# Moving one block's shared chunks across a tile run, and its next routing behind them

## The chip, the cores and the metric

The kernel runs on one core of a Trainium2 chip. The metric is the device time of one execution in microseconds (us). Five engines take part: TensorE (PE, matrix products), VectorE (DVE), ScalarE (ACT), GpSimd (POOL; here it issues the indirect DMAs) and SyncE (SP; it issues the plain DMAs). Each runs its own program in order, and they meet only through semaphores.

## The reference

Input x has 2 x 1024 tokens of 256 features, all in float32. Six steps follow each other; LN is a layer norm without gain:

```
x = x + 0.5 * moe0(LN(x))      # feed-forward 0 (f = 0)
x = x + rwkv_block(LN(x))      # mixing
x = x + 0.5 * moe0(LN(x))      # f = 1, same weights as f = 0
x = x + 0.5 * moe1(LN(x))      # f = 2
x = x + linear_attention(LN(x))
x = x + 0.5 * moe1(LN(x))      # f = 3

def moe(x):                    # moe0: 8 experts, top 2, width 176, softmax scores
    scores = f(x @ gate_w)     # moe1: 32 experts, top 6, width 96, sigmoid scores
    routed = sum over the chosen experts e of w_e * ((silu(x @ wg[e]) * (x @ wu[e])) @ wd[e])
    shared = (silu(x @ sg) * (x @ su)) @ sd      # width 352 in moe0, 192 in moe1
    return routed + shared
```

So the routing of f = 2 for a token needs everything that f = 1 adds to that token: its shared part and both of its routed parts.

## The kernel before, in words

**Data.** The tokens are 16 tiles of 128, in 4 blocks of 512 (NB = 4, NT = 4). XT holds x in on-chip memory throughout. Each feed-forward has two parts:

- The *shared* part is computed in *chunks*: 3 per block for f = 0 and 1 (SH0), 2 per block for f = 2 and 3. For one chunk TensorE does `gate_up` (L794, 12 matmuls of 128x512, matmul at L817), ScalarE `silu` (L1375), VectorE `prod` (L2037), ScalarE `hidden` (L1381), VectorE `low_hidden` (L2044), and TensorE `down` (L820, 12 matmuls, L829). Each operand is split into a high and a low half, which is why there are so many steps. When a block's last `down` is done, VectorE adds it into XT (`finish`, L2049, instruction at L2061), which raises the semaphore CK.sum.
- The *routed* part works on *pages*. For each block the router makes statistics (`stats`), normalised rows (`rows`), a transposition (`turn`, L757), logits (L1026), scores (`score`, L1366), the chosen experts (`chosen`, L1891), ranks (L774) and slots (`slots`, L1932). POOL then scatters the rows into DRAM pages by slot (`scatter_tile`, L626; one indirect DMA per tile and choice, so 8 per block for f = 1 and 24 for f = 2). Pages are sorted by expert. The *tile run* (`tiles`, on TensorE L864) loads pairs of pages (20 pairs for f = 1), multiplies them with their expert's weights and writes them to DRAM. It can start only when every block is scattered. POOL gathers the results (`gather`, L645) and VectorE adds them into XT (`gathered`, L2072).

**The order around the change** is written out by hand, engine by engine.

1. *Mixing.* After its last step stands a drain, the list DRAIN (L125): the 9 shared chunks of f = 1 of blocks 0, 1 and 2 (`LATE = 3` blocks). Between chunks the routing of f = 1 for blocks 2 and 3 is done. Block 3's slots come after the sixth chunk.
2. *Tile run of f = 1.* TensorE waits for the sum of block 2 (L1338). Beside the pairs the engines route blocks 0 and 1 for f = 2 (`route_ahead`, `route_between`, `route_beside`) and VectorE gathers blocks 0, 1 and 2. At pair 19 VectorE makes the f = 2 statistics of block 2. SyncE loads five groups of the f = 2 expert weights at pairs 4 to 8 (`next_weights`, L567); these groups lie over memory that the mixing has finished with.
3. *`prepare2`.* The 3 held chunks of block 3 run between the steps of block 2's routing. VectorE then makes block 2's slots, adds block 3's sum, gathers block 3, makes block 3's statistics, and the 8 shared chunks of f = 2 run between the steps of block 3's routing.
4. *Tile run of f = 2.* SyncE waits for all scatters (L494) before the first page load.

POOL's own order (L721 to L744) is: gathers of f = 1 with the scatters of tiles 0 to 4 of f = 2 between them, then the scatters of tiles 5 to 15; the scatter of a block's first tile waits for the block's slots.

The chunks that run inside the mixing or its drain are of kind "s0" and those behind the tile run of kind "d0"; the kind chooses the buffers of S and HL only, which for "d0" lie over the expert weights of f = 0 and 1.

## Time and profile before

| | us |
|---|---|
| median of 3 runs | 1507.77 (1500.41, 1507.77, 1521.20) |
| the profiled execution | 1497.55 |
| its span in the profile | 1495.7 |
| TensorE busy in the span | 1178.6 (79%) |
| VectorE busy | 743.8 (50%) |
| POOL busy | 596.8 (40%) |
| ScalarE busy | 536.0 (36%) |

The span is what the profile shows of the profiled execution, and the other times are read inside it, in us from its start. A busy share is an average over all stages and says nothing of a single one. In a row of the timeline the bracket at the end is the time that the engine was idle before, and what released it; "remote" there is a release that the profile can't lay to a recorded instruction.

### The profile page before, as it was taken

Reading aid. Unit: us, or ns where it says so; the run is one execution under the profiler, and the core shown is the slowest. Engines: PE = TensorE matmul, PEld = TensorE weight load, DVE = VectorE, ACT = ScalarE, POOL = GpSimd, SP = SyncE. Lnnn points to the kernel's source line nnn. Section 1 sums busy time; section 2 is a strip of 40 time slices with the busy share of each in tenths; the row PEclk is TensorE's granted clock in tenths of the full one; section 3 lists DMA queues with packets and bytes.
Section 4 is the critical chain, followed back from the end, with each engine's and each line's share of the span. In section 5 each row is a group of like instructions: output and inputs, shape, how many; then the busy total and the mean of one; then the engine's idle time right before and its main releaser. Section 6 shows DMA issues by size and latency. Waiting matters only on the chain.

```text
span 1495.7 us, 20198 instructions
## 1 busy us (share of the span) xinstructions
PE 1178.6 (79%) x6031; PEld 960.0 (64%) x6031; DVE 743.8 (50%) x2333; ACT 536.0 (36%) x1012; POOL 596.8 (40%) x579
## 2 busy tenths in 40 slices
PE   4799988979989898854768998897755436988884
PEld 4677755666778676633557987875434225978784
DVE  5553465564546536413445555678644214633443
ACT  2323344554533234321413433442303115644442
POOL 3661352211124213674550155662453730045554
PEclk9789999998989999865868999898875667998897
DMA  9523439400002573331426687760121212676676
GB/s 331 211 72 107 143 96 308 141 1 0 1 29 107 206 260 119 117 114 64 173 76 216 195 241 237 219 191 4 60 79 41 105 53 63 198 208 205 204 223 191
DMA packets 125302, 209.81 MB, mean 140 GB/s; under 512 B 15296, under 2 KB 104768, under 8 KB 123328
## 3 DMA queue, kind: packets, MB, share of 16 engines
q1 hardware_dynamic: 100624, 141.38, 28.7%
q0 software_dynamic: 24576, 67.14, 14.4%
q8 instruction: 56, 0.92, 0.3%
q14 instruction: 46, 0.38, 0.1%
HBM read 129.29 MB, written 101.19 MB: 154 GB/s over the span
## 4 chain that ended last, share of the span: by engine, by line
PE 48%; DVE 18%; issue 13%; another core or an unknown queue 10%; ACT 6%; POOL 3%; DMA 1%; SPq 0%; DVEq 0%; POOLq 0%; ACTq 0%
PE ps L910 15%; PE ps L932 6%; PE ps L877 5%; PE ps L817 4%; PE ps L829 4%; PE ps L889 3%; PE ps L1093 2%; PE ps L1100 2%; ACT xnt L1360 1%; PE ps L927 1%; PE ps L1244 1%; DVE HL L2047 1%; POOL xd L638 1%; PE ps L925 1%
## 5 line engine op out<-in xcount | busy, mean ns | idle before, releaser
L653 POOL DMA_INDIRECT G<-yd,slot_of x256 | 253.1, 989 | 424.6 <-issue 189.3
L638 POOL DMA_INDIRECT xd<-xnt,slot_of x256 | 251.4, 982 | 224.4 <-DVE slot_of L1986 136.9
L910 PE MATMUL ps<-WE,xT 128*128 x1016 | 200.7, 343 | 5.6 <-issue 3.9
L2102 DVE TENSOR_TENSOR hid<-hid,ps 128x192 f32<-128x192 f32 (+2 forms) x168 | 65.4, 389 | 247.9 <-ACT hid L1551 198.1
L910 PEld LDWEIGHTS ps<-WE,xT 128*128 128x128 f32 x1016 | 174.0, 202 | 9.9 <-issue 9.7
L1522 ACT ACTIVATE xT<-ps 128x512 f32<-128x512 f32 (+1 forms) x168 | 99.2, 590 | 156.9 <-PE ps L877 121.6
L877 PE MATMUL ps<-ident,xd_in 128*128 128x128 f32 x664 | 108.2, 287 | 44.2 <-ACT xT L1522 24.0
L2081 DVE SCALAR_TENSOR_TENSOR XT<-G,wt,XT 128x256 f32<-128x256 f32 x256 | 123.8, 494 | 27.5 <-DMA G<-yd,slot_of 17.0
L1551 ACT ACTIVATE hid<-ps 128x192 f32<-128x192 f32 (+2 forms) x168 | 60.4, 359 | 192.1 <-PE ps L910 139.9
L877 PEld LDWEIGHTS ps<-ident,xd_in 128*128 128x128 f32 x664 | 84.5, 148 | 60.6 <-issue 37.0
L1379 ACT ACTIVATE S<-ps 128x512 f32<-128x512 f32 (+1 forms) x72 | 42.6, 592 | 179.1 <-PE ps L817 140.1
L910 PE MATMUL ps<-W0E,xT 128*128 x312 | 103.3, 475 | 0.1
L2109 DVE COPY yo<-ps 128x512 f32<-128x512 f32 x104 | 70.9, 682 | 59.6 <-PE ps L932 30.7
L2047 DVE TENSOR_TENSOR HL<-S,HL 128x512 fp32r<-128x512 f32 (+1 forms) x72 | 51.9, 721 | 92.8 <-ACT HL L1388 87.0
L817 PE MATMUL ps<-XH,W0S 128*128 128x512 f32 x288 | 87.5, 456 | 8.9 <-issue 7.1
L932 PE MATMUL ps<-W0E,hT 88*128 x312 | 80.0, 401 | 13.3 <-issue 10.0
L889 PE MATMUL ps<-ident,hid 128*96 128x128 f32 (+1 forms) x410 | 75.5, 282 | 17.1 <-issue 7.6
L1388 ACT ACTIVATE HL<-S 128x512 fp32r<-128x512 f32 (+1 forms) x72 | 45.0, 625 | 104.8 <-DVE S L2042 70.7
L932 PEld LDWEIGHTS ps<-W0E,hT 88*128 88x128 f32 x312 | 61.6, 200 | 29.0 <-issue 15.1
L761 PE MATMUL ps<-ident,xnt 128*128 128x128 f32 x232 | 40.4, 332 | 50.3 <-ACT xnt L1360 41.3
L817 PEld LDWEIGHTS ps<-XH,W0S 128*128 128x128 f32 x288 | 62.7, 224 | 26.3 <-issue 12.0
L910 PEld LDWEIGHTS ps<-W0E,xT 128*128 128x128 f32 x312 | 58.7, 198 | 28.3 <-issue 5.1
(245 smaller groups left out, 2173.6 us busy)
## 6 DMA issues: line engine op xcount, KB each, us to landing
xd_in<-xd SPq DMA_DIRECT2D x164, 256.0 KB
yd<-yo SPq DMA_DIRECT2D x164, 256.0 KB
WE<-w SPq DMA_DIRECT2D x8, 1280.0 KB
W0E<-w0e SPq DMA_DIRECT2D x1, 4864.0 KB
xd<-xnt,slot_of POOLq DMA_INDIRECT x256
G<-yd,slot_of POOLq DMA_INDIRECT x256
W0E<-w0e SPq DMA_DIRECT2D x1, 3040.0 KB
XT<-x_in SPq DMA_DIRECT2D x4, 512.0 KB, 6.1
```

The source lines that it names most:

```text
L638: nc.gpsimd.indirect_dma_start(xd[f // 2][:, :], bass.IndirectOffsetOnAxis(ap=slot_of[:, t, k:k + 1], axis=0), xnt[:, t, :], None).then_in ...
L653: nc.gpsimd.indirect_dma_start(G[:, n % G_RING, :], None, yd[f // 2][0:min(ly.early[t][k] * 2, ly.TILES) * P, :], bass.IndirectOffsetOnAxi ...
L817: last = mm(ps[0:ch.H, ch.bank + u, :], l, r, start=(i == 0), stop=(i == len(terms) - 1))
L877: last = nc.tensor.transpose(ps[:, TX, (2 * a + k) * P:(2 * a + k + 1) * P], xd_in[:, q % X_RING, a, k * P:(k + 1) * P], ident[:, :])
L889: last = nc.tensor.transpose(ps[0:ly.part, hth, n * P:(n + 1) * P], hid[:, q % 2, a, c * ly.part:(c + 1) * ly.part], ident[:, :])
L910: last = mm(dst, xT[:, q % 2, a, k, :], flat[:, bass.ds(expert[2 * q + a] + k * 2 * ly.H, 2 * ly.H)], start=(k == 0), stop=(k == KD - 1))
L932: last = mm(ps[:, ty, a * D:(a + 1) * D], hT[0:ly.part, q % 2, a * ly.parts + c, :], flat[0:ly.part, bass.ds(expert[2 * q + a] + ly.down_a ...
L1522: fn(xT[:, q % 2, 0:m].rearrange("p a k t -> p (a k t)"), ps[:, TX, 0:m * D], ACT.Copy).then_inc(TL.xT, 1)
L2047: tt(hl[0:ch.H, 1, ch.i % 2, :], S_of[ch.kind][0:ch.H, ch.i % 2, :], hl[0:ch.H, 0, ch.i % 2, :].bitcast(F32), ALU.subtract).then_inc(CK.lo, 1)
L2081: stt(XT[:, t, :], G[:, n % G_RING, :], wt[:, t, k:k + 1], XT[:, t, :], ALU.mult, ALU.add).then_inc(g_used, 1)
L2102: tt(hid[:, q % 2, 0:m, 0:ly.H], hid[:, q % 2, 0:m, 0:ly.H], src, ALU.mult).then_inc(TL.hid, 1)
L2109: copy(yo[:, q % Y_RING, 0:m].rearrange("p a d -> p (a d)"), ps[:, down_bank(f, q), 0:m * D]).then_inc(TL.y, 1)
```

## The change

`HELD = 2` is new. The drain holds only the chunks of blocks 0 and 1, the tile run of f = 1 waits for the sum of block 1 only, and the chunks of block 2 become of kind "d0" and run behind the tile run in `prepare2`, ahead of block 3's. In `prepare2` the six chunks now run first, one behind the other, and the routing of block 2 for f = 2 begins when block 2's sum is in XT (after the sixth gate_up on TensorE). VectorE's statistics of block 2 move from pair 19 to behind that sum, and its gathers of what is left of block 3 stand before the slots of block 2 and not behind them. VectorE may gather tiles of block 3 inside the tile run. Weight group 7 of f = 2 overlaps the operand of block 2's chunks and is loaded behind the last sum, with groups 0, 1 and 6.

```diff
+HELD = 2
@@ chunk_table
-    for b, banks in enumerate(((2, 2, 2), (2, 6, 2), (6, 2, 6), (2, 6, 2))):
-        add(("s", 1, b), "s0" if b < LATE else "d0", 1, b, SH0, banks)
+    for b, banks in enumerate(((2, 2, 2), (2, 6, 2), (2, 6, 2), (6, 2, 6))):
+        add(("s", 1, b), "s0" if b < HELD else "d0", 1, b, SH0, banks)
-DRAIN = [ch for b in range(LATE) for ch in RUN["s", 1, b][0]]
+DRAIN = [ch for b in range(HELD) for ch in RUN["s", 1, b][0]]
@@ SyncE, next_weights
-                    sp.wait_ge(CK.sum, GROUP["s", 1, LATE - 1] + 1)
+                    sp.wait_ge(CK.sum, GROUP["s", 1, HELD - 1] + 1)
-                if 4 <= i < 9:
-                    expert_weights((2, 3, 4, 5, 7)[i - 4])
+                if 4 <= i < 8:
+                    expert_weights((2, 3, 4, 5)[i - 4])
...
             sp.wait_ge(CK.sum, GROUP["s", 1, 3] + 1)
-            for g in (0, 1, 6):
+            for g in (0, 1, 6, 7):
@@ TensorE, prepare2
-                held = RUN["s", 1, LATE][0]
+                held = RUN["s", 1, 2][0] + RUN["s", 1, 3][0]
                 pe.wait_ge(TL.hid, PAIR0[2])
                 pe.wait_ge(TL.hT, PAIR0[2])
                 gate_up(held[0], taken_over(held[0]))
                 pe.wait_ge(TL.y, PAIR0[2])
+                for k in range(1, 6):
+                    gate_up(held[k], taken_over(held[k]))
+                    down(held[k - 1])
                 route_turn(2)
-                gate_up(held[1], taken_over(held[1]))
+                down(held[5])
                 route_logits(2)
-                down(held[0])
-                gate_up(held[2], taken_over(held[2]))
-                down(held[1])
                 route_rank(2)
-                down(held[2])
                 chunk(0)
@@ TensorE, before the tile run of f = 1
-            pe.wait_ge(CK.sum, GROUP["s", 1, LATE - 1] + 1)
+            pe.wait_ge(CK.sum, GROUP["s", 1, HELD - 1] + 1)
@@ ScalarE, prepare2
+                for k in range(4):
+                    silu(held[k])
+                    hidden(held[k])
                 std(F_NORM[2], 2)
+                silu(held[4])
+                hidden(held[4])
                 routed_rows(2)
-                silu(held[0])
+                silu(held[5])
+                hidden(held[5])
                 route_plain(2)
-                hidden(held[0])
-                silu(held[1])
                 score(2, 2, A_BANK)
-                hidden(held[1])
-                silu(held[2])
-                hidden(held[2])
@@ VectorE, gathered
-                    if (f, t // NT) != (0, LATE):
+                    if f >= 2 or t // NT < (LATE, HELD)[f]:
@@ VectorE, route_beside
-                if i == 19:
-                    route_stats(2)
@@ VectorE, prepare2
+                for k in range(4):
+                    prod(held[k])
+                    low_hidden(held[k])
+                finish(held[2])
+                dve.wait_ge(CK.sum, GROUP["s", 1, 2] + 1)
+                route_stats(2)
                 offsets(F_NORM[2], 2, True)
-                prod(held[0])
-                low_hidden(held[0])
-                prod(held[1])
+                for k in (4, 5):
+                    prod(held[k])
+                    low_hidden(held[k])
+                finish(held[5])
                 chosen(2, 2)
-                low_hidden(held[1])
-                prod(held[2])
-                low_hidden(held[2])
+                gathered_all(1, first)
                 route_slots(2)
-                finish(held[2])
-                gathered_all(1, first)
+                dve.wait_ge(CK.sum, GROUP["s", 1, 3] + 1)
                 route_stats(3)
@@ VectorE, the tile run of f = 1
-            m = tiles(1, 2, 2, route_beside, route_ahead, route_between, NB - 1)
+            m = tiles(1, 2, 2, route_beside, route_ahead, route_between)
```

## Rows read from the trace of the kernel before

**Rows 1.** The page's first line.
```profile
span 1495.7 us, 20198 instructions
```
**Rows 2.** Stretches: length, busy us of each engine (instructions), granted clock, DMA share, GB/s.
```profile
500.00:520.00 20.00, 17.34 (x91) 13.36 (x90) 6.21 (x9) 4.06 (x7) 5.37 (x5) 0.91 0.48 146
...
640.00:660.00 20.00, 9.95 (x26) 7.08 (x24) 2.89 (x11) 1.98 (x3) 15.13 (x17) 0.59 0.34 114
...
700.00:720.00 20.00, 7.12 (x27) 5.30 (x27) 14.40 (x48) 0.00 (x0) 9.08 (x9) 0.59 0.59 228
```
**Rows 3.** Timeline, drain's end: start, us, engine, line, operation, out<-in, count [idle before].
```profile
495.84 0.18 DVE L1986 TENSOR_SCALAR slot_of<-v 128x32 int32<-128x32 f32 x1
...
503.89 2.91 PE L817 MATMUL ps<-XH,W0S 128*128 128x512 f32 x12
...
505.72 0.96 POOL L638 DMA_INDIRECT xd<-xnt,slot_of  x1 [0.30 <-issue]
...
508.20 7.08 SPq L545 DMA_DIRECT2D xd_in<-xd  x5
...
512.84 1.23 DVE L2061 SCALAR_TENSOR_TENSOR XT<-ps,XT 128x1024 f32<-128x1024 f32 x1 [2.31 <-PE ps L829]
...
514.26 0.63 PE L877 MATMUL ps<-ident,xd_in 128*128 128x128 f32 x4 [1.15 <-DVE XT L2061]
```
**Rows 4.** Timeline of TensorE, the first two pairs' gate and up.
```profile
516.44 4.23 PE L910 MATMUL ps<-W0E,xT 128*128 x8
...
522.25 2.53 PE L910 MATMUL ps<-W0E,xT 128*128 x8
```
**Rows 5.** Timeline, routing of block 2 for f = 2.
```profile
647.82 1.39 DVE L1839 BATCH_NORM_STATS2 st<-XT 128x6 f32<-128x256 f32 x4
...
661.23 0.20 ACT L1354 ACTIVATE rs<-rs 128x4 f32<-128x4 f32 x1 [8.85 <-remote]
...
671.17 1.02 ACT L1445 ACTIVATE X<-ps 128x1024 f32<-128x1024 f32 x1 [3.65 <-remote]
...
672.25 2.69 PE L1031 MATMUL ps<-graw,X 128*128 128x32 f32 x16 [1.56 <-ACT X L1445]
...
687.87 0.97 POOL L638 DMA_INDIRECT xd<-xnt,slot_of  x1 [0.30 <-issue]
...
690.17 3.11 PE L817 MATMUL ps<-XH,W0S 128*128 128x512 f32 x5 [1.51 <-issue]
...
692.34 0.28 ACT L1373 ACTIVATE sc<-ps 128x128 f32<-128x128 f32 x1 [10.05 <-remote]
...
705.71 0.18 DVE L1986 TENSOR_SCALAR slot_of<-v 128x32 int32<-128x32 f32 x1
...
707.63 4.07 DVE L2081 SCALAR_TENSOR_TENSOR XT<-G,wt,XT 128x256 f32<-128x256 f32 x8
```
**Rows 6.** Timeline, block 3 and the start of the third tile run.
```profile
714.99 8.58 PE L817 MATMUL ps<-XHe,WS 128*96 128x512 f32 x24 [12.88 <-issue]
...
732.03 1.87 PE L1031 MATMUL ps<-graw,X 128*128 128x32 f32 x16
...
739.58 0.97 POOL L638 DMA_INDIRECT xd<-xnt,slot_of  x1 [0.30 <-issue]
...
741.88 0.28 ACT L1373 ACTIVATE sc<-ps 128x128 f32<-128x128 f32 x1 [3.57 <-remote]
...
755.84 0.18 DVE L1986 TENSOR_SCALAR slot_of<-v 128x32 int32<-128x32 f32 x1
...
760.04 2.93 PE L829 MATMUL ps<-WS,HL 96*128 96x256 f32 x12 [3.79 <-DVE HL L2047]
...
788.59 1.91 SPq L545 DMA_DIRECT2D xd_in<-xd  x4
...
791.78 1.08 PE L877 MATMUL ps<-ident,xd_in 128*128 128x128 f32 x4 [11.58 <-DVE emap L2015]
```
**Rows 7.** Timeline, a chunk's sum in the preparation of f = 3.
```profile
1218.49 1.22 DVE L2061 SCALAR_TENSOR_TENSOR XT<-ps,XT 128x1024 f32<-128x1024 f32 x1 [32.95 <-remote]
```

More of the change, by code:

```diff
@@ L1468, in chunk @@
                     hidden(chunks[k])
-                held = RUN["s", 1, LATE][0]
+                held = RUN["s", 1, 2][0] + RUN["s", 1, 3][0]
                 act.wait_ge(TL.down, PAIR0[2])
+                for k in range(4):
+                    silu(held[k])
+                    hidden(held[k])
                 std(F_NORM[2], 2)
+                silu(held[4])
+                hidden(held[4])
                 routed_rows(2)
-                silu(held[0])
+                silu(held[5])
+                hidden(held[5])
                 route_plain(2)
-                hidden(held[0])
-                silu(held[1])
                 score(2, 2, A_BANK)
-                hidden(held[1])
-                silu(held[2])
-                hidden(held[2])
                 route_split(0)
@@ L2229, in route_beside @@
                     route_stats((i - 10) // 4)
-                if i == 19:
-                    route_stats(2)
             def prepare2(first):
-                NG = LY[0].NG
-                assert first == 3 * NG
+                assert first >= 3 * LY[0].NG
                 chunks = [ch for b in range(NB) for ch in RUN["s", 2, b][0]]
@@ L2240, in chunk @@
                     low_hidden(chunks[k])
-                held = RUN["s", 1, LATE][0]
+                held = RUN["s", 1, 2][0] + RUN["s", 1, 3][0]
+                for k in range(4):
[4 more added lines that the diff above has]
+                route_stats(2)
                 offsets(F_NORM[2], 2, True)
-                prod(held[0])
-                low_hidden(held[0])
-                prod(held[1])
+                for k in (4, 5):
+                    prod(held[k])
+                    low_hidden(held[k])
+                finish(held[5])
                 chosen(2, 2)
-                low_hidden(held[1])
-                prod(held[2])
-                low_hidden(held[2])
+                gathered_all(1, first)
                 route_slots(2)
-                finish(held[2])
-                gathered_all(1, first)
+                dve.wait_ge(CK.sum, GROUP["s", 1, 3] + 1)
                 route_stats(3)
```

## The prediction

> **What bounds the kernel now.** I read the page first: the profiled execution took 1497.55 us, its span is 1495.7 us [rows 1], and the share of busy TensorE over the whole says little about one stage. So I read busy time in stretches of 20 us [rows 2]: TensorE works all but 3 us of 500 to 520, half of 640 to 660, and 7.1 us of 700 to 720, with VectorE at 14.4. Around the change the kernel has three stages: the end of the mixing (about 480 to 512), the tile run of the second feed-forward (514 to 661), and the preparation of the third one (661 to 792).
>
> The timeline of the first stage's end [rows 3] shows two things that finish almost together. Slots of block 3 are known at 495.84, the last of its 8 scatters starts at 505.72 (one every 1.3 us or so), and SyncE sends the first page loads at 508.20. The three shared chunks of block 2 run meanwhile and are summed into XT at 512.84 + 1.23 = 514.1; the tile run's first transpose is at 514.26. The last thing waited for is the chunks, but only by 3 us.
>
> The preparation is a serial routing chain with TensorE mostly as its servant. Block 2's statistics begin at 647.82, inside the tile run; the chain goes on at 661.23, when the last pair is through, and the logit matmuls are recorded at 672.25 [rows 5]. ScalarE gets them at 692.34, after a wait of 10.05 us. Slots come at 705.71, and only then do 8 gathers and block 3's statistics follow. For block 3: first new chunk 714.99, logits recorded 732.03, scored 741.88, slots 755.84, page loads 788.59, first transpose of the third tile run 791.78 [rows 6]. So tile run 3 starts 35.9 us after block 3's slots, since 24 scatters stand between. POOL does nothing from 689 until slots 2, and again from 741 until slots 3.
>
> **The holds.** In both cases the logits were recorded long before ScalarE had them, and it had them when POOL's series of scatters was over: series last started at 687.87, score at 692.34 [rows 5]; 739.58 and 741.88 [rows 6]. The sum at 1218.49 waited 32.95 us for matmuls in a third such series [rows 7]. I call this a hold: TensorE's results come late while a series of indirect DMAs is being issued. Not every result in a series is late, so where a hold falls after the change is the main unknown.
>
> **The change, part by part.**
>
> *Three chunks leave the drain.* Each is 12 gate-and-up matmuls (2.91 us at full clock, row at 503.89) and 12 down matmuls. At most the start moves from 514.3 to the landing of the first pages. Those are sent at 508.20 and depend on scatters that the change does not touch; at 788.59 to 791.78 such a load was in and used within 3.2 us [rows 6]. So the start is 511.4 at the latest and the gain about 3 us, not the 13.5 us that three chunks take at 2.91 + 1.6. Against it: TensorE now idles from about 501 (six chunks done) to 511, and the granted clock of 500 to 520 was already 0.91. The first pair's eight expert matmuls took 4.23 us, the next pair's 2.53 [rows 4]; one more such slow pair costs about 2 us, none costs 0. I take 3 us gained, bounds 0 and 3.
>
> *The tile run.* One weight load of 1280 KB leaves SyncE's queue at pair 8 and goes behind the run; what stood behind it in the queue (page loads, sends) comes at most about 1 us sooner. The run's end hangs on waits for POOL, DMA and routing (640 to 660 is half idle, rows 2), so nothing is taken for it. VectorE drops block 2's statistics (2 us) at pair 19 and may do two gathers more there; both fit into its wait for the last pair. POOL's order is the same. The last-pair time stays 661.2, less 3.
>
> *Six chunks before block 2's routing.* Here the order turns over. Until now statistics (647.82) preceded everything and routing began at 661.2 with one chunk beside each step. Now routing of block 2 starts only when its own shared sum is in XT, which needs gate_up of four chunks, down of three, and one sum. Working times: two gate_ups at the lower clock took 8.58 us, 4.3 each [rows 6]; down takes 2.93 [rows 6] at the lower clock and, from half of that, about 1.6 at the higher.
>
> Before, by 693.3 (690.17 + 3.11) TensorE had done three gate_ups, one transposition, logits and one down. POOL's scatters of block 1 (until 687.87) are the same after the change, so I assume the same amount by 693.3: three gate_ups and two downs. Then gate_up 4.3 and down 2.9 bring 700.5; the sum takes 1.2 (as at 512.84) and statistics 2.2 (1.39 in the row at 647.82, 0.8 by my estimate for the small steps behind it), beside which TensorE does gate_up 4.3, down 2.9, and with the clock back up gate_up 2.9 and down 1.6: 712.2. Transposition 1.1 (as at 791.78), down 1.6, logits 1.9 (732.03), one copy of 1.02 (671.17) and as much for a handover bring the logits to 718.8; ScalarE's silus and row passes lie beside that. From score to slots was 13.4 us (692.34 to 705.71); the 8 gathers at 4.07 us in all that now stand ahead of the slots take the place of what rank waited for. Slots 2 are at 732.2, less 3 is 729, against 705.7: **23 us later**.
>
> *Block 3.* Its statistics follow at once, without gathers and sum. The first new chunk was 9.3 us after slots 2 and is now 4.0. Logits would be recorded 17.0 us after it. Without a hold, slots 3 are at 729 + 4.0 + 17.0 + 1.9 + 14.0 = 766. With a hold to the end of the series: 24 scatters at 1.3 us (755.84 to the page loads at 788.59 holds such a series and its landing) from 729 end at 760, score 2 us later, and 14.0 more (741.88 to 755.84): 776. I take the held value because both series of the preparation had a hold at just this step. The third tile run starts 35.9 us after slots 3: 812, against 791.8. **Sum: +20 us**, bounds +10 (no hold at block 3) and, if slots 2 come later, more.
>
> *Weights.* Four loads instead of three go out after block 3's sum (about 717). They are through by 732 and the run needs them at 811: nothing. They no longer collide with block 2's series, which may save it 3 us; the held time above has that in it.
>
> From the third tile run on nothing is changed, and no later wait is known that would give the 20 us back.
>
> Against the profiled execution: 1497.55 + 20 = 1517.6 us. The timed runs lie at 1500 to 1521 with the median 10 us above the profiled one; set on the median, 1507.8 + 20 = **1528 us**, +1.3%. About 2%, 30 us, is what a measurement of this kernel can tell from no change.
>
> **Rivals.**
>
> *A, the forecast (0.50).* Holds stay where series are; +20.
>
> *B, the first hold goes (0.22).* If TensorE is not held between 663 and 692, gate_up 4.3, down 2.9, gate_up 4.3, down 2.9, gate_up 2.9, down 1.6 end at 680.8 instead of 700.5. Slots 2 are then at 709, the series collides with weights again and ends at 743, held score and slots 3 at 760: +4, so 1512 us. For it: during the series of 706 to 740 two gate_ups ran at a normal 8.58 us. Against it: logits recorded at 672.25 were not with ScalarE before 692.34, and 20 us are no clock effect.
>
> *C, no holds at all: faster (0.10).* Slots 2 at 709, logits not held, slots 3 at 709 + 37 = 746, behind block 2's series at 743: the third run starts 10 us earlier than before, 1498 us. It decides from the point at which the gate_ups of block 2 and 3 leave no idle TensorE in 661 to 692. The step itself is possible, since TensorE was fed too little there.
> The Trainium skill (Runtime: NRT & Kernel Launch, Instruction fetch mechanics) has each engine's sequencer fetch the next block of instructions by its own DMA in the background and calls the crossing mostly hidden; by that, a straight run of chunks should not be held at all and this rival should be the likeliest. The trace speaks against it with waits of 10.05 and 32.95 us on matmuls recorded long before, so I leave it at one in ten.
>
> *D, a longer hold (0.15).* If nothing but the first gate_up gets through until the series ends at 692, 14.4 us of work (two gate_ups, two downs at the lower clock) come on top: +34, 1542 us. This is also where silu and hidden of four chunks, all ahead of block 2's rows on ScalarE, would show as late.
>
> *E (0.03).* The change does nothing visible: the drain's 3 us and a partial shift cancel, or the tile run itself moves by more than I can see.
>
> **Numbers.** Likeliest 1528. The range leaves out half of C and part of D: 1502 to 1545. Faster by over 2% (below 1478) is in none of the cases: 0.03. Slower by over 2% (above 1538) is D and the upper edge of A: 0.20. Within 2%: 0.77.
>
> **What would show it.** Right: first transpose of the second tile run near 511; XT sum of block 2 near 700, statistics behind it; slots 2 near 729 and slots 3 near 776, POOL idle between 687 and 729; third run's first transpose near 812. Wrong: slots 2 before 715 (B or C), slots 3 less than 40 us behind slots 2 (no second hold), the tile run's last pair moved by more than 5 us from 658, or a start of the second run still at 514, which would mean that pages and not chunks were last.

## The result, and the profile after

The changed kernel took 1524.22 us (median of 12 runs, 1514.69 to 1537.06), the kernel before 1514.38 us beside it (median of 12, 1495.24 to 1524.3). The ratio of the fast runs alone, which leaves out the longest runs of the kernel before, is 1.0108, 95% interval 1.0076 to 1.0141, or about 16 us; the two medians differ by 9.8 us. So there is a small loss, between 10 and 16 us. The profiled execution took 1526.47 us. From here on instructions behind the new line 32 have a line number higher by one or more (L2061 is now L2062, the gather's sum L2081 is L2082), and the experiments' numbers drift by a few more; the operand names say which instruction it is.

The page's first line, then stretches of 20 us (length, busy us of PE, PEld, DVE, ACT, POOL with the number of instructions, granted clock, DMA share, GB/s):

```profile
span 1524.7 us, 20198 instructions
```
```profile
500.00:520.00 20.00, 7.71 (x40) 5.92 (x40) 4.36 (x22) 1.83 (x3) 7.67 (x8) 0.76 0.43 144
640.00:660.00 20.00, 8.94 (x21) 6.70 (x22) 1.90 (x4) 1.29 (x3) 15.35 (x16) 0.51 0.35 116
700.00:720.00 20.00, 11.08 (x69) 9.96 (x68) 12.58 (x50) 10.21 (x15) 0.00 (x0) 0.76 0.46 184
```

Against [rows 2], TensorE's 17.3 us of work in 500 to 520 are 7.7: three chunks have left. In 640 to 660 nothing has changed much, and in 700 to 720 TensorE is busy for 11.1 us instead of 7.1, since the rest of block 3's six chunks and block 2's transposition, logits and ranks now run there.

**The drain and the start of the tile run** (timeline: start, us, engine, line, operation, out<-in, count [idle before]), to be read against [rows 3] and [rows 4]:

```profile
500.60 0.18 DVE L1987 TENSOR_SCALAR slot_of<-v 128x32 int32<-128x32 f32 x1
...
505.14 1.22 DVE L2062 SCALAR_TENSOR_TENSOR XT<-ps,XT 128x1024 f32<-128x1024 f32 x1 [1.78 <-issue]
...
509.90 0.96 POOL L639 DMA_INDIRECT xd<-xnt,slot_of  x1 [0.30 <-issue]
...
512.39 4.44 SPq L546 DMA_DIRECT2D xd_in<-xd  x5
...
515.35 1.09 PE L878 MATMUL ps<-ident,xd_in 128*128 128x128 f32 x4 [9.94 <-DMA xd_in<-xd]
...
518.10 3.89 PE L911 MATMUL ps<-W0E,xT 128*128 x8
...
523.57 2.53 PE L911 MATMUL ps<-W0E,xT 128*128 x8
```

The sum is done at 506.4, the last scatter starts at 509.90, and the transpose now waits 9.94 us for pages, not for a sum. Slots were 4.8 us later than before (500.60 against 495.84) although nothing changed ahead of them: executions differ by that much, and 4.1 us of it are there at the first gather already. From slots to the first transpose it is 14.75 us against 18.42 before, so the shorter drain gives back 3.7 us, and three chunks, 13.5 us of TensorE, vanish from it. The first yo copy of the run (a pair's result on its way to DRAM), behind the slow first pair, has 3.4 us of it left.

**Block 2's routing** in `prepare2`, against [rows 5]:

```profile
663.15 0.43 DVE L2110 COPY yo<-ps 128x256 f32<-128x256 f32 x1 [10.30 <-remote]
...
674.56 2.91 PE L818 MATMUL ps<-XH,W0S 128*128 128x512 f32 x12
...
677.30 1.60 PE L830 MATMUL ps<-W0S,HL 128*128 128x256 f32 x12
...
678.74 1.55 PE L818 MATMUL ps<-XH,W0S 128*128 128x512 f32 x6
...
682.02 0.49 PE L818 MATMUL ps<-XH,W0S 128*128 128x512 f32 x1 [0.20 <-issue]
682.72 0.48 PE L818 MATMUL ps<-XH,W0S 128*128 128x512 f32 x1 [0.21 <-issue]
...
684.17 0.39 PE L818 MATMUL ps<-XH,W0S 128*128 128x512 f32 x1 [0.97 <-issue]
...
690.00 0.97 POOL L639 DMA_INDIRECT xd<-xnt,slot_of  x1 [0.30 <-issue]
692.64 0.60 ACT L1379 ACTIVATE S<-ps 128x512 f32<-128x512 f32 x1 [16.50 <-remote]
...
695.26 1.22 DVE L2062 SCALAR_TENSOR_TENSOR XT<-ps,XT 128x1024 f32<-128x1024 f32 x1
...
708.28 1.87 PE L1032 MATMUL ps<-graw,X 128*128 128x32 f32 x16
...
710.19 0.28 ACT L1373 ACTIVATE sc<-ps 128x128 f32<-128x128 f32 x1 [1.58 <-PE ps L1032]
...
721.72 0.18 DVE L1987 TENSOR_SCALAR slot_of<-v 128x32 int32<-128x32 f32 x1
```

The third `down`, which completes block 2's shared part, runs at 677.30. The sum stands behind the fourth chunk's `prod` and `low_hidden` in VectorE's order, and the fourth gate_up is held: it is recorded in one piece at 674.56, but ScalarE has its result only at 692.64, after 16.50 us, 2.6 us behind the start of the last scatter. The third `down` itself is held as well: its matmuls end at 678.9 by the record, but among the semaphore events of the trace its signal, for which the sum waits, stands at 694.11, only 1.2 us ahead of the sum. Of the fifth gate_up the last matmuls are recorded singly, 0.7 and 1.4 us apart. So the sum is at 695.26, and slots 2 at 721.72, 16.0 us later than before. The logits are no longer held: POOL has nothing to issue by then.

**Block 3 and the third tile run**, against [rows 6]:

```profile
745.42 1.57 PE L1032 MATMUL ps<-graw,X 128*128 128x32 f32 x9 [3.48 <-ACT X L1445]
...
750.69 0.21 PE L1032 MATMUL ps<-graw,X 128*128 128x32 f32 x1 [1.88 <-issue]
...
752.11 0.97 POOL L639 DMA_INDIRECT xd<-xnt,slot_of  x1 [0.30 <-issue]
754.20 0.21 PE L1032 MATMUL ps<-graw,X 128*128 128x32 f32 x1 [1.90 <-issue]
...
756.32 0.59 ACT L1379 ACTIVATE S<-ps 96x512 f32<-96x512 f32 x1 [10.01 <-remote]
...
759.43 0.63 ACT L1388 ACTIVATE HL<-S 96x512 fp32r<-96x512 f32 x1 [2.52 <-DVE S L2043]
...
761.37 0.28 ACT L1373 ACTIVATE sc<-ps 128x128 f32<-128x128 f32 x1
...
774.93 0.18 DVE L1987 TENSOR_SCALAR slot_of<-v 128x32 int32<-128x32 f32 x1
...
811.17 1.08 PE L878 MATMUL ps<-ident,xd_in 128*128 128x128 f32 x4 [10.31 <-DVE emap L2016]
...
1251.18 1.23 DVE L2062 SCALAR_TENSOR_TENSOR XT<-ps,XT 128x1024 f32<-128x1024 f32 x1 [32.29 <-remote]
```

Here the hold can be watched: nine logit matmuls run at full pace, then single ones with up to 1.9 us between them, until shortly after the last scatter of the series (752.11). The logits are through at 755.1, and their signal stands at 756.58. ScalarE scores them 4.8 us later, without idle time: a chunk's `silu` and `hidden` stand ahead of the score in its order, and the `silu` waited 10.01 us for its own held gate_up. Slots 3 come 53.2 us behind slots 2 (before: 50.1), and the third tile run starts at 811.17 against 791.78, 19.4 us later, of which 4.8 stood ahead of the change. That is 14.6 us net; the timed runs say 10 to 16. The last row is the counterpart of [rows 7], the same wait in the preparation of f = 3.

The profiled pair differs by 29 us in the end. The other 9.5 arise inside the third tile run, in which nothing was changed: its first 41 yo copies take 121.4 us before, 132.4 after, and 123.7 to 134.7 in the experiments e1 to e6, on either side of the change alike. So I take them for variation of executions and not for an effect.

### The profile page after: what moved, and what is told of

It reads as the page before. It is cut to its first block, busy times and chain, and to the rows that moved or that the text cites. A ratio compares the mean times of both kernels' runs of the same rounds, so it can differ in the third digit from the quotient of the medians.

```text
span 1524.7 us, 20198 instructions
## 1 busy us (share of the span) xinstructions
PE 1174.4 (77%) x6031; PEld 956.2 (63%) x6031; DVE 743.6 (49%) x2333; ACT 536.1 (35%) x1012; POOL 595.4 (39%) x579
## 4 chain that ended last, share of the span: by engine, by line
PE 46%; DVE 16%; issue 13%; another core or an unknown queue 12%; ACT 6%; POOL 3%; DMA 2%; SPq 1%; POOLq 0%; ACTq 0%; DVEq 0%
PE ps L911 14%; PE ps L933 6%; PE ps L818 5%; PE ps L878 4%; PE ps L830 3%; PE ps L890 2%; PE ps L1093 2%; PE ps L1100 2%; ACT xnt L1360 1%; PE ps L1244 1%; DMA G<-yd,slot_of 1%; POOL xd L639 1%; DVE HL L2048 1%; PE ps L762 1%
## 5 line engine op out<-in xcount | busy, mean ns | idle before, releaser
L911 PEld LDWEIGHTS ps<-WE,xT 128*128 128x128 f32 x1016 | 176.0, 204 | 15.2 <-issue 14.7
L2082 DVE SCALAR_TENSOR_TENSOR XT<-G,wt,XT 128x256 f32<-128x256 f32 x256 | 123.5, 493 | 27.6 <-DMA G<-yd,slot_of 16.4
L911 PEld LDWEIGHTS ps<-W0E,xT 128*128 128x128 f32 x312 | 58.6, 198 | 28.5 <-issue 5.1
```

The costliest lines, as they stand in the source:

```text
L911: last = mm(dst, xT[:, q % 2, a, k, :], flat[:, bass.ds(expert[2 * q + a] + k * 2 * ly.H, 2 * ly.H)], start=(k == 0), stop=(k == KD - 1))
L2082: stt(XT[:, t, :], G[:, n % G_RING, :], wt[:, t, k:k + 1], XT[:, t, :], ALU.mult, ALU.add).then_inc(g_used, 1)
```

## The experiments

In the expectations and below, slots 2 and slots 3 are the f = 2 slots of blocks 2 and 3. The times of each kernel are read against its own last yo copy of the second tile run (661.2 before, 663.2 after), as this takes out what happened earlier. It is not free of holds itself: that copy waited 11.40 us before, 10.30 in the changed kernel, 4.64 in e3 and 1.43 in e6. There is one trace of each kernel. The ratios are to the kernel before, timed beside each.

| kernel | ratio (95%) | slots 2 behind that copy, us |
|---|---|---|
| before | 1 | 44.5 |
| changed | 1.0108 (1.0076 to 1.0141) | 58.6 |
| e1, changed, old routing place | 1.0052 (1.0013 to 1.009) | 38.6 |
| e2, changed, block 2's chunks gone | 1.0028 (0.9996 to 1.0061) | 43.1 |
| e3, changed, one pause | 1.012 (1.0078 to 1.0163) | 79.2 |
| e4, before, pauses for logits | 0.9952 (0.9919 to 0.9985) | 38.4 |
| e5, before, short drain | 0.995 (0.9909 to 0.9991) | 38.7 |
| e6, before, pauses for rank | 0.9915 (0.988 to 0.995) | 23.8 |
| e7, before, pause every 12 scatters | 0.971 (0.9655 to 0.9764) | 50.1 |
| e8, before, every 6 | 0.9675 (0.9631 to 0.9719) | 24.8 |
| e9, e8 without block 3's | 0.9586 (0.9543 to 0.9628) | 24.6 |
| e10, changed, e9's pauses | 0.9568 (0.9511 to 0.9626) | 49.0 |
| e11, before, e9's and in f = 0, 1 | 0.9492 (0.944 to 0.9545) | 24.9 |
| e12b, changed, e11's pauses, other chip | 1.042 (1.04 to 1.0441) | 41.8 |

### e1: the routing of block 2 back at its old place

```diff
@@ TensorE, prepare2
-                for k in range(1, 6):
+                route_turn(2)
+                gate_up(held[1], taken_over(held[1]))
+                route_logits(2)
+                down(held[0])
+                gate_up(held[2], taken_over(held[2]))
+                down(held[1])
+                route_rank(2)
+                for k in range(3, 6):
                     gate_up(held[k], taken_over(held[k]))
                     down(held[k - 1])
-                route_turn(2)
                 down(held[5])
-                route_logits(2)
-                route_rank(2)
@@ VectorE, route_beside
+                if i == 19:
+                    route_stats(2)
@@ VectorE, prepare2
...
-                dve.wait_ge(CK.sum, GROUP["s", 1, 2] + 1)
-                route_stats(2)
...
```

Statistics are made at pair 19 again, so the router doesn't see block 2's shared part. ScalarE and the rest of VectorE follow the same order.

> The changed kernel with block 2's routing put back where it was (statistics at pair 19, rows, transposition, logits and slots between the first chunks), the six chunks still behind the tile run. Block 2's routing then does not see its own shared part, which is the part of the computation that is changed. Theory 'late routing' (the cost is that block 2's slots wait for its sum): slots 2 return to about 1 to 4 us of their old place, slots 3 come some 12 us later than slots 3 before at most, since three more chunks (13 us) still stand ahead of block 3's statistics; time ratio to before 0.998 to 1.007. Rival 'volume' (six chunks crowd the preparation whatever the order): ratio stays at 1.009 to 1.013.

Measured: 1505.33 us, the kernel before 1498.54, ratio 1.0052. Slots 2 come 38.6 us behind the last pair instead of 58.6 (44.5 before), and of the change's 1.1% about half is gone, as forecast, though the intervals of the two ratios overlap. The silu of block 2's third chunk is what is held in this kernel (a wait of 16.29 us, until 689.24), the logits are not (scored at 670.85). Slots 3 then come 63.7 us behind slots 2, against 53.2 in the changed kernel, with the other three chunks between them. So the late routing does cost, but only part of what it moves arrives at the end.

### e2: the three chunks left out

```diff
...
-        add(("s", 1, b), "s0" if b < HELD else "d0", 1, b, SH0, banks)
+        if b != 2:
+            add(("s", 1, b), "s0" if b < HELD else "d0", 1, b, SH0, banks)
...
-                held = RUN["s", 1, 2][0] + RUN["s", 1, 3][0]
+                held = RUN["s", 1, 3][0]
...
```

Block 2's shared part of f = 1 is computed nowhere. TensorE does block 3's three gate_ups and two downs ahead of block 2's transposition, and VectorE makes the statistics behind the first of the three chunks.

> The changed kernel without block 2's three shared chunks of the second feed-forward (they are not computed anywhere). Routing order as in the changed kernel. 'Late routing': what is left is that statistics follow the run instead of preceding it, but the wait for six gate_ups is gone, so slots 2 at 705 to 712 and ratio to before 0.993 to 1.000. Rival 'volume': the same direction, since the volume is gone too; together with e1 it gives the price of the three chunks in their new place, which I put at 13 to 20 us of span against the changed kernel.

Measured: 1499.69 us, ratio 1.0028. Without the chunks the routing comes at about the time of before (43.1 us behind the last pair, 44.5 before). The ratio is above the forecast range of 0.993 to 1.000, since this time the transposition's result is held, for 12.12 us, and the logits follow it:

```profile
686.35 1.02 ACT L1446 ACTIVATE X<-ps 128x1024 f32<-128x1024 f32 x1 [12.12 <-remote]
686.58 0.97 POOL L640 DMA_INDIRECT xd<-xnt,slot_of  x1 [0.30 <-issue]
```

The moved chunks cost about 12 us, then, as the difference of the ratios (0.008 x 1514); what the rest of the change costs, less what the short drain gives, can't be told from zero.

### e3 and e4: POOL waits for the logits

```diff
             for t in range(5, TT):
+                if t == 11:                       # e3; e4: t in (6, 11)
+                    pool.wait_ge(RT.logits, NB * 2 + NB)    # e4, t == 6: NB * 2 + 3
                 scatter_tile(2, t)
```

e3 is on the changed kernel, e4 on the kernel before, where block 1's last twelve scatters wait likewise for block 2's logits.

> The changed kernel; POOL waits for block 3's logits before the last 6 of block 2's 24 scatters. Theory 'hold' (TensorE crawls as long as a series of indirect DMAs goes on): logits come 3 to 10 us after POOL stops at about 744 and not at 756, slots 3 at 762 to 766 and not at 775, 10 to 14 us less than the changed kernel, ratio to before 1.000 to 1.005. Rival (the lateness has another cause, for instance TensorE's own instruction supply): logits still come at 753 or later, the last 6 scatters start later still, and the time is the same or up to 8 us longer.

> The kernel before with the same pause, and one more: POOL waits for block 2's logits after the first 6 of the 18 scatters of block 1. 'Hold': block 2's logits come 1 to 8 us after POOL's stop at about 673 and not at 692, slots 2 at 688 to 695 and not at 706; block 3's logits no longer wait for the series; 15 to 25 us less, ratio 0.983 to 0.990. Rival: no change or up to 15 us longer, since scatters wait for logits that are late for another reason.

Measured: e3 1513.87 us, ratio 1.012; e4 1487.74, ratio 0.9952. In e3 slots 3 come 44.7 us behind slots 2 instead of 53.2, so the hold at block 3 was worth about 8.5 us. But in front of slots 2 this execution was held longer, and nothing is left of the gain that was forecast (ratio 1.000 to 1.005):

```profile
681.61 0.60 ACT L1381 ACTIVATE S<-ps 128x512 f32<-128x512 f32 x1 [31.20 <-remote]
```

That wait ends in the middle of the series of 668.35 to 690.58, and another `silu` waits 13.40 us until 696.99. e4 also missed its range of 0.983 to 0.990, though it gains a little. Its logits of block 2 are through at 679.74, with the next chunk held in their place:

```profile
676.35 1.86 PE L1033 MATMUL ps<-graw,X 128*128 128x32 f32 x16
...
679.74 0.28 ACT L1375 ACTIVATE sc<-ps 128x128 f32<-128x128 f32 x1 [1.29 <-remote]
...
694.44 0.97 POOL L638 DMA_INDIRECT xd<-xnt,slot_of  x1 [0.30 <-issue]
698.10 0.60 ACT L1381 ACTIVATE S<-ps 128x512 f32<-128x512 f32 x1 [16.26 <-remote]
```

A pause at one point doesn't remove the hold; what TensorE does later in the series gets it, here until 3.7 us behind the start of the last scatter.

### e5: the short drain alone

```diff
+        if b != 2:
+            add(("s", 1, b), "s0" if b < LATE else "d0", 1, b, SH0, banks)
-DRAIN = [ch for b in range(LATE) for ch in RUN["s", 1, b][0]]
+DRAIN = [ch for b in range(2) for ch in RUN["s", 1, b][0]]
...
```

The kernel before with two blocks in the drain; block 2's shared part of f = 1 is computed nowhere. The tile run waits for block 1's sum, as in the changed kernel.

> The kernel before with a drain of two blocks: block 2's three shared chunks of the second feed-forward are not computed anywhere, all routing stays in its old order. This is the gain side of the change alone. My prediction took 3 us for it (the pages, not the chunks, then start the tile run): ratio to before 0.996 to 1.000. Rival 'the drain was the bound': the 13.5 us of the three chunks come off, ratio 0.989 to 0.993.

Measured: 1504.11 us, the kernel before 1512.56, ratio 0.995, or 7.5 us with an interval from 1 to 14. Its tile run too starts on pages:

```profile
502.01 1.23 DVE L2062 SCALAR_TENSOR_TENSOR XT<-ps,XT 128x1024 f32<-128x1024 f32 x1 [1.79 <-issue]
...
512.21 1.08 PE L878 MATMUL ps<-ident,xd_in 128*128 128x128 f32 x4 [9.93 <-DMA xd_in<-xd]
```

From slots (497.5) to the transpose it is 14.7 us, as in the changed kernel. The ratio lies between the two forecasts. The 3 to 4 us of the trace are within the interval, and the 13.5 us of the rival just inside its other end; it is the trace that tells them apart.

### e6: block 1's last scatters wait for block 2's rank

```diff
+                if t == 6:
+                    pool.wait_ge(RT.ranked, NB * 2 + 3)
+                if t == 11:
+                    pool.wait_ge(RT.logits, NB * 2 + NB)
```

> The kernel before; POOL waits after the first 6 of block 1's 18 scatters until block 2's ranks are through on TensorE, and in block 2's series for block 3's logits as in e4. If late results are due to POOL's series, nothing on block 2's way from rows to slots is held now: slots 2 within 26 us of the last pair (before 44, e4 38), slots 3 within 48 us of slots 2, 12 to 20 us less than before, ratio 0.987 to 0.992. Rival (lateness has another cause): slots 2 stay 36 us or more behind the last pair and the ratio is 0.995 or more.

Measured: 1494.03 us, ratio 0.9915. Six scatters, a gap of 5.74 us, then the other twelve, with the rank and slots done in the gap and behind it: slots 2 come 23.8 us behind the last pair. This is the length of the old routing chain without a hold, and it puts block 2's hold in the kernel before at 44.5 - 23.8 = 20.7 us. Slots 3 come 55.0 us behind slots 2 and not within the 48 forecast: a sum in block 2's series waits 10.57 us.

### e7, e8 and e9: POOL waits until its scatters have landed

```diff
+                if f >= 2 and t % 2 == 1:         # e7; e8: every t; e9: every t < 12
+                    scattered_upto(pool, GATHER0[f] + (t + 1) * ly.K)
```

> The kernel before; in the feed-forwards of 32 experts POOL waits after every 12 scatters until all of them have landed, about 2 us each time. If a hold needs a long unbroken series (before, the series of 31 us ran 19 to 27 us before results came late), holds shrink: the sum that waited 32.95 us comes within 15, ratio 0.985 to 0.995. Rival (it is the number of scatters or their traffic, not the unbroken series): waits of the same length, ratio 1.000 to 1.008 from the pauses.

> As e7 with a wait after every 6 scatters. If unbroken series make the holds, they are gone altogether (no result later than 5 us after its matmuls), at a price of up to 8 us of pauses in each block's series that lies on the path: ratio 0.985 to 1.000. Rival: holds as before and the pauses on top, ratio 1.005 to 1.015.

> As e8 (the kernel before, POOL waits for landing after every 6 scatters in the feed-forwards of 32 experts), but without the waits in block 3's 24 scatters, which in e8 end last and alone. The theory 'unbroken series make the holds, pauses cost about 3.3 us each': third tile run 15 to 35 us earlier than in e8, fourth one 10 to 20 us earlier; ratio to before 0.935 to 0.955. Rival: the unbroken series of block 3 brings the holds back onto chunks that are still to be done, ratio 0.965 or more.

Measured: 1465.25 us (ratio 0.971), 1460.93 (0.9675) and, beside another set of runs of before (1513.7), 1450.81 (0.9586). All three are on the kernel before and compute the same. POOL's timeline in e8, between two waits:

```profile
748.17 0.97 POOL L638 DMA_INDIRECT xd<-xnt,slot_of  x1 [0.30 <-issue]
751.48 0.97 POOL L638 DMA_INDIRECT xd<-xnt,slot_of  x1 [2.34 <-issue]
```

Each wait costs POOL about 2 us (2.34 idle instead of 0.30). For this the sum in the preparation of f = 3 that waited 32.95 us [rows 7] waits 3.02, in the midst of scatters:

```profile
1143.18 1.22 DVE L2063 SCALAR_TENSOR_TENSOR XT<-ps,XT 128x1024 f32<-128x1024 f32 x1 [3.02 <-PE ps L831]
```

From block 0's to block 3's slots of f = 3 it is 73.4 us in e8 and 109.2 before: 36 us, most of the gain. The tile run of f = 1, beside which scatters of f = 2 are issued, is 118.8 us from first to last yo copy and not 134.7. The preparation of f = 2 gains nothing: from the last pair to the third tile run it takes 130.5 us before, 140.8 in e8 and 134.0 in e9. From 640 to 1260 no wait laid to "remote" is over 6 us in e8, POOL's left out. e7 and e8 gained more than forecast. e9's ratio lies just above its range of 0.935 to 0.955, and its third tile run starts 10 us earlier than e8's and not 15 to 35. e9 leaves block 3's scatters unbroken, since nothing but the page loads stands behind them.

### e10: the changed kernel with e9's pauses

```diff
+                if f >= 2 and t < 12:
+                    scattered_upto(pool, GATHER0[f] + (t + 1) * ly.K)
```

> The changed kernel with the same pauses as e9. It tells how much of the change's price comes from holds. 'Late routing' alone (block 2's routing starts behind four gate_ups and three downs, 15 to 20 us, whatever POOL does): e10 is 10 to 18 us longer than e9, slots 2 some 15 us later behind the last pair. Rival 'it was holds that the six chunks ran into': e10 within 4 us of e9.

Measured: 1444.34 us against e9's 1450.81, ratios 0.9568 and 0.9586, equal within their intervals. I had held it more likely that the changed kernel would again be 10 to 18 us longer, and that was wrong. Slots 2 are 21.2 us later (693.80 against 672.62), yet the third tile run starts earlier. In e9, then in e10:

```profile
718.76 0.18 DVE L1988 TENSOR_SCALAR slot_of<-v 128x32 int32<-128x32 f32 x1
...
776.42 0.97 POOL L638 DMA_INDIRECT xd<-xnt,slot_of  x1 [0.30 <-issue]
...
781.96 1.09 PE L879 MATMUL ps<-ident,xd_in 128*128 128x128 f32 x4 [43.32 <-DMA xd_in<-xd]
```
```profile
734.94 0.18 DVE L1989 TENSOR_SCALAR slot_of<-v 128x32 int32<-128x32 f32 x1
...
771.50 0.97 POOL L639 DMA_INDIRECT xd<-xnt,slot_of  x1 [0.30 <-issue]
...
777.02 1.09 PE L880 MATMUL ps<-ident,xd_in 128*128 128x128 f32 x4 [22.71 <-DMA xd_in<-xd]
```

In e9 slots 3 are known at 718.76 and the last scatter starts 57.7 us later; an unbroken series of 24 takes 30. POOL is what sets the end, and TensorE waits 43.32 us for pages. In e10 16 us of lateness go into that wait. From the last pair to the third tile run it is 134.0 us in e9 and 132.2 in e10, against 130.5 and 148.0 without pauses. The changed order is a loss only as long as the routing chain is the last thing waited for.

### e11: pauses in f = 0 and 1 too

```diff
+                if t < 12 and (f >= 2 or t % 3 == 2):
+                    scattered_upto(pool, GATHER0[f] + (t + 1) * ly.K)
```

> As e9, with pauses after every third tile (6 scatters) in the two feed-forwards of 8 experts as well, again not in block 3. There results were late by 11 us once (at 62 us of the span) and by 6 us once (at 481). If those are the same holds: ratio 0.003 to 0.010 below e9. Rival: the pauses delay the first scatter series, nothing gained, e11 within 0.002 of e9 or above it.

Measured: 1435.16 us against 1513.7 for the kernel before, ratio 0.9492, the lowest of all and just inside the forecast, though its interval overlaps e9's. It is the kernel before plus this wait.

### e12b: the same on the changed kernel

> The changed kernel with the same pauses as e11 (POOL waits until all its scatters have landed after every tile in f = 2 and 3 and after every third tile in f = 0 and 1, in both for the tiles of blocks 0 to 2 only). e11, the same on the kernel before, had the ratio 0.949 to before. Theory: behind block 2's series POOL, now with pauses, sets the end of the preparation, and both kernels end equal there (e9 and e10: slots of block 2 at 672.6 and 693.8, third tile run at 781.9 and 777.0). Then this kernel has slots 2 some 20 us later than e11's 665.5, the third tile run within 6 us of e11's, and a ratio of 0.944 to 0.954. Rival, that routing behind the chunks costs its 16 us also here (the equality of e9 and e10 was luck of the two compilations): ratio 0.957 to 0.962.

Measured: 1357.59 us, with the kernel before at **1302.43** us (nine runs, 1299.97 to 1306.45), ratio 1.042. Neither theory had this. The run fell on another chip than the others, and there the kernel before is 13 to 14% shorter than the 1498 to 1514 us measured elsewhere, and the changed kernel with pauses is 4.2% longer. There is no trace of the kernel before from that chip, so this ratio can't be split into the change and the pauses, and whether that kernel has holds there is unknown. What the trace of e12b shows is the changed `prepare2` with no hold in it, timeline:

```profile
634.07 0.42 DVE L2112 COPY yo<-ps 128x256 f32<-128x256 f32 x1
...
643.86 2.91 PE L820 MATMUL ps<-XH,W0S 128*128 128x512 f32 x12
...
646.81 0.60 ACT L1381 ACTIVATE S<-ps 128x512 f32<-128x512 f32 x1 [2.19 <-PE ps L820]
...
649.43 1.22 DVE L2064 SCALAR_TENSOR_TENSOR XT<-ps,XT 128x1024 f32<-128x1024 f32 x1
...
662.40 1.87 PE L1034 MATMUL ps<-graw,X 128*128 128x32 f32 x16
...
675.84 0.18 DVE L1989 TENSOR_SCALAR slot_of<-v 128x32 int32<-128x32 f32 x1
```

The fourth gate_up starts at 643.86 and ScalarE has its result at 646.81, so the sum comes 15.4 us behind the last pair instead of 32.1. With e11 this gives the table that the prediction lacked, slots 2 behind the last pair: old order 24.9 us without a hold and 44.5 with one, changed order 41.8 and 58.6. Both orders carry a hold of 17 to 20 us; the change adds 14 to 17 with or without it. (e10 has 49.0, with the sum 15.4 us behind the last pair as in e12b, but with a wait of 6.76 us for the transposition.) The third tile run starts 134.1 us behind the last pair in e12b and 135.1 in e11 (first transposes at 768.19 and 775.65), so the rest of the expectation, equal ends under pauses, is met in the trace, if from two chips.

## Why the prediction was right, and where it was off

**The drain.** Forecast 3 us, between 0 and 3. The trace has 3.7 at the first transpose, just above that bound, and 3.4 at the first yo copy, and pages are waited for (e5 too). The page loads went out 11.8 us behind slots and not 12.4, and were in use after 3.0 us and not 3.2. So it was right that the chunks were last by 3 us only, and right that their 13.5 us of work is no gain.

**The tile run.** Nothing was taken for it, and from its first to its last yo copy it takes 135.3 us after and 134.7 before. But its last pair was then forecast at 658.2 and came at 663.2, since the profiled execution began 4.8 us late.

**Block 2's routing.** Forecast slots 2 at 729, 23 us later; measured 721.7, 16 us later. Two terms of that sum were too large. The first is the state at 693.3: I took three gate_ups and two downs as done and charged a gate_up of 4.3 and a down of 2.9 behind it. In the trace four gate_ups and three downs are recorded by 678.9, and their results are there with the hold's end: the fourth gate_up's at 692.6, the third down's at 694.1. From last pair to sum it is 32.1 us and not 39.3, and the 7.2 between them are the size of these two terms. The second is the chain from the sum to slots: 26.5 us, not 31.7, with ScalarE scoring 14.9 us behind the sum (forecast 18.3) and slots 11.5 behind that (13.4 from [rows 5]). The later last pair took 5 of the 12 back. The direction and the reason stand: e1, which puts the routing back, brings slots 2 to 38.6 us, and e12b beside e11 gives the order's own price, 17 us, from one trace each and two chips. That the hold would stay in 663 to 692 was right. Rival B had no hold there and slots 2 at 709, 50.8 us behind its last pair; e12b has 41.8, so that chain, too, was priced too long.

**Block 3.** Forecast 47 us from slots 2 to slots 3 with a hold, measured 53.2. The hold is there, on the logits, as named, and on a chunk's gate_up besides. But the logits were scored 9.3 us behind the start of the last scatter and not 2: 4.5 us until their signal, as the last of them run singly until 755, and 4.8 more for the `silu` and `hidden` that stand ahead of the score on ScalarE and were late too, which the sum did not have. With slots 2 seven us early and this six us late, slots 3 came at 774.9 against 776, and the third tile run at 811.2 against 812. The end of the stage was right by two errors that nearly cancel.

**Weights.** Forecast nothing. The four loads go out at 709.74, 101 us ahead of the third tile run, and from 700 to 1040 no wait is laid to them. No run leaves them alone out; in e2, with the same four loads behind the sum, all effects together are 1.0028 with 1 in the interval.

**Nothing gives it back.** Right: 14.6 us net at the third tile run, 10 to 16 us in the timed runs. The sum said 20, with 10 as its lower bound. That 1524 us came of the 1528 is in part luck: the kernel before took 1514.4 us beside the change and not the 1507.8 of three runs on which the 20 were set, and these 6.6 us hide as much of the shortfall. The timed runs also tell more than the 2% that the prediction allowed them: the interval of the ratio is 0.3% to either side.

**The assumption under it all**, that results of TensorE come late while POOL issues a long series of indirect DMAs, was taken from three rows. e7 to e11 support it strongly: when POOL stops for landing every six scatters, those waits are gone or short on this kernel (sums of all waits laid to "remote" from 640 to 1260, POOL's left out: 211 us before, 248 after, 58 in e8, 41 in e11). In the preparation of f = 2 the pauses also move the series: in e9 block 2's slots (672.62) are there before block 1's last 18 scatters begin (672.96), so there the missing hold can be due to either; the sum at 1143.18 in e8 is the clean case. And a hold does not always last to the end of its series. The kernel before has one of 22.76 us that ends 29 us ahead of the last scatter (1213.44), as the 31.20 us in e3 do 9 us ahead:

```profile
1184.18 0.63 ACT L1388 ACTIVATE HL<-S 96x512 fp32r<-96x512 f32 x1 [22.76 <-remote]
1184.33 0.96 POOL L638 DMA_INDIRECT xd<-xnt,slot_of  x1 [0.30 <-issue]
```

The assumption is tied to the chip, though, as e12b and its 1302 us suggest. What delays TensorE is open. The Trainium skill (Runtime: NRT & Kernel Launch, Instruction fetch mechanics) calls the cost of going on to the next fetched block of instructions mostly hidden. The packets of the larger of the two instruction queues take a median of 1.0 us both in the traces with holds and in e12b, so nothing here shows it slower, and they do not stand at the holds' ends in any fixed way (at 656.8, 705.7 and 753.2 in the changed kernel, with holds that end at 692.6 and 756.3). The Trainium skill (SBUF — State Buffer, SBUF: two separate sides) says that compute engines and DMAs don't slow each other in that memory; the traces neither confirm nor contradict this, since the matmuls' own durations stay 0.21 to 0.49 us in a hold, and it is the gaps between them that grow.

A version that was not tried: block 2's sum ahead of the fourth chunk's `prod` on VectorE. The matmuls of the third `down` were done at 678.9 by the record, 16 us before the sum, but as their signal stands at 694.11, little more than 1 us would be won.

## What to carry to other kernels

Ahead of moving work out of a drain, ask what the drain's end waits for next: 13.5 us of chunks were worth 3.7, because pages were almost as late. Ahead of moving work in front of a serial chain, price the move at what the chain's first step then waits for, which here was four gate_ups and three downs and not the six chunks: the sum came 15.4 us behind the last pair without a hold (e10, e12b) and 32.1 with one; and when a second resource, such as POOL with its pauses, ends later than the chain, the same move is free. Where a profile has long "remote" waits on finished matmuls during a series of indirect DMAs, let the issuing engine wait for landing every six or so and measure it, on more than one chip: it gave 5% on one, and on another, where it was run on the changed order alone, the two together lost 4%.

## What the runs showed of the hardware that was not expected

- A wait until six scatters have landed costs POOL about 2 us (2.34 idle instead of 0.30) and shortened the kernel by 3.3% (e8), 4.1% (e9) and 5.1% (e11).
- A matmul's record can stand 15 us ahead of its signal: the third `down` of the changed kernel ends at 678.9 and signals at 694.11.
- In a hold TensorE's records thin out: logit matmuls of 0.21 us start 0.7 us or multiples of it apart (747.16, 747.88, 748.60, 750.69, 752.09, 754.20), and results or full pace are back 2.3 to 5.8 us behind the last scatter's start (741.88 behind 739.58 before; 1251.18 in the changed kernel). Some holds end earlier, in mid-series (22.76 us before, 31.20 in e3).
- One pause isn't enough: the hold moves to the next thing that TensorE does in the series (e3, e4).
- The same kernel before took 1498.54, 1512.56 and 1513.7 us in three sets of runs on three chips and 1302.43 in a fourth set on another, with the granted clock at 0.86 to 0.88 in the former and 0.92 to 0.93 in the latter. Packets of POOL's queue take a median of 159 ns in the trace of the kernel before and in that of e12b, from the fourth chip. Why one chip is so much quicker isn't settled.
